# A state-space layer whose convolution becomes three shifted projections, with the row scaling moved to ScalarE

## The reference, cut to what matters

```python
xz = x @ W_in.T
u, z = jnp.split(xz, 2, axis=-1)
uc = conv(u over time, conv_w, 3 taps, padding 1, each of 256 channels by itself)
uc = silu(uc + conv_b)
...                                # delta, B and C from uc, a scan over time for 16 states
y = y * silu(z)
return y @ W_out.T

h = gelu(x_flat @ W1[e] + b1[e])   # for each of 8 experts e and the shared one
out = sum_e combine[e] * (h @ W2[e] + b2[e])
```

## Time and profile before

| what | value |
|---|---|
| runs | 2823.01, 2826.26, 2810.18 us, median 2823.01 |
| profiled execution | 2826.37 us, span 2824.6 us |
| granted TensorE clock over the span | 0.876 of full speed |
| start to the first step of loop 0 | 71 us |
| loops 0 to 3 | 71 to 937 us |
| rest of the mixture of batch 3 | 937 to 1097 us |
| attention | to about 2170 us |
| last layer | to the end |

### The profile page before, as it was taken

The page is one execution under the profiler, slowest core; times in us unless marked ns, Lnnn a source line. Parts: engine busy times, 40 slices in busy tenths (PEclk is TensorE's granted clock), DMA queues, the critical chain, the costliest instruction groups (busy, mean ns, idle before and its releaser), DMA issues.

```text
span 2824.6 us, 42372 instructions
## 1 busy us (share of the span) xinstructions
PE 2196.3 (78%) x15570; PEld 1492.3 (53%) x15570; DVE 2127.1 (75%) x3677; ACT 1699.0 (60%) x2627; POOL 1528.9 (54%) x1343
## 2 busy tenths in 40 slices
PE   2433788588589697989889888989896799739877
PEld 1101456255356475656556566656664568536665
DVE  4999978978978514999999999999998431572344
ACT  5353666477457344989888888888894134212422
POOL 0435323523433202878987887788788524553146
PEclk7555889698689898999999999999997899869988
DMA  3000000000000000110000000011010000000000
GB/s 108 0 0 0 1 0 1 1 1 1 19 1 1 18 6 12 34 25 23 24 24 24 24 24 23 24 30 28 24 35 23 1 1 1 1 15 1 1 1 16
DMA packets 32032, 42.06 MB, mean 15 GB/s; under 512 B 8897, under 2 KB 18130, under 8 KB 31442
## 3 DMA queue, kind: packets, MB, share of 16 engines
q1 hardware_dynamic: 31826, 39.34, 5.2%
HBM read 12.05 MB, written 2.10 MB: 5 GB/s over the span
## 4 chain that ended last, share of the span: by engine, by line
PE 37%; DVE 35%; ACT 12%; issue 8%; POOL 7%; SPq 0%; DMA 0%; POOLq 0%; ACTq 0%; DVEq 0%
DVE MA L1300 11%; PE ps L862 7%; DVE WB L1309 5%; PE ps L791 3%; ACT HR L763 3%; PE ps L793 2%; PE ps L792 2%; PE ps L1161 2%; PE ps L1132 2%; PE ps L1985 2%; DVE lnb L317 2%; DVE BIG L336 2%; ACT BIG L448 2%; DVE BIG L342 2%; PE ps L1144 2%
## 5 line engine op out<-in xcount | busy, mean ns | idle before, releaser
L1300 DVE TENSOR_REDUCE MA<-ps 128x1 f32<-128x1024 f32 x512 | 606.3, 1215 | 42.6 <-PE ps L1132 38.5
L420 POOL TENSOR_TENSOR MA<-MA,BIG 128x1024 f32<-128x1024 f32 x128 | 299.0, 2357 | 544.1 <-DVE BIG L342 544.1
L1228 ACT ACTIVATE WB<-ps,MA 128x1024 f32<-128x1024 f32 x461 | 513.4, 1117 | 114.9 <-DVE MA L1300 102.6
L1132 PE MATMUL ps<-BIG 96*128 96x512 f16 x1024 | 316.1, 391 | 95.3 <-ACT WB L1228 84.3
L1380 POOL TENSOR_SCALAR WB<-WB,MA 128x384 f32<-128x384 f32 x256 | 371.1, 1450 | 8.5
L862 PEld LDWEIGHTS ps<-WB,HR 128*128 128x128 f32 x2304 | 291.6, 202 | 33.8 <-issue 16.7
L862 PE MATMUL ps<-WB,HR 128*128 128x128 f32 x2304 | 300.4, 288 | 8.7 <-DVE acc L707 8.5
L763 ACT ACTIVATE HR<-ps,b 128x512 f32<-128x512 f32 x288 | 190.2, 686 | 148.9 <-PE ps L793 148.0
L1732 POOL TENSOR_TENSOR BIG<-MA,BIG 128x512 f32<-128x512 f32 x128 | 132.9, 1048 | 229.6 <-PE ps L1971 76.1
L1144 PE MATMUL ps<-ident,WB 128*128 128x128 f32 x1640 | 226.2, 282 | 9.8 <-DVE WB L1309 5.7
L1383 POOL TENSOR_TENSOR WB<-WB 128x384 f32<-128x384 f32 x205 | 209.3, 1021 | 17.1
(11 more groups left out here) (294 smaller groups left out, 4962.3 us busy)
## 6 DMA issues: line engine op xcount, KB each, us to landing
BIG<-BIG SPq DMA_DIRECT2D x192, 64.0 KB, 2.0
BIG<-MA SPq DMA_DIRECT2D x192, 64.0 KB, 2.0
WB<-w_dram SPq DMA_DIRECT2D x1, 2304.0 KB, 14.9
X<-x_dram SPq DMA_DIRECT2D x4, 512.0 KB, 12.6
HR<-w_dram SPq DMA_DIRECT2D x1, 2048.0 KB, 9.5
out_dram<-X SPq DMA_DIRECT2D x4, 512.0 KB, 3.2
BIG<-wqkv_dram SPq DMA_DIRECT2D x1, 1536.0 KB, 6.2
WB<-w_dram SPq DMA_DIRECT2D x2, 512.0 KB, 5.1
```

Of the source, the lines that this page charges most:

```text
L420: e.tensor_tensor(yy[:, c, :], yy[:, c, :], db[n % 2][c], ALU.add).then_inc(*p_my.up(b, n, c))
L1132: x = e.matmul(ps[s][:, 512 * h:512 * h + 512], stack[q % 2][0:96, 0, 2 * pp + s, 128 * i:128 * i + 128], stack[q % 2][0:96, 1, 2 * pp + s ...
L1228: e.activation(P_of(n, s), ps[s][:, :], ACT.Exp, bias=L[:, 2 * s + pp:2 * s + pp + 1], scale=1.0, accum_out=L[:, 4 + 2 * s + pp:5 + 2 * s ...
L1300: e.tensor_reduce(L_of(n)[:, c:c + 1], ps[s][:, :], AX, ALU.max, negate=True).then_inc(*v_amx.up(n, s))
```

## The change

**The convolution.** A new input `cwr` holds the taps as three rows, each broadcast to all partitions by a DMA of its own. At the start POOL multiplies the projection's weights with them into three sets of weights, `taps`. Each of the four tiles of u is then three matmuls that accumulate in PSUM, two of them on x shifted by one column; ACT copies the result with the bias straight into `cv`, and silu reads that. The padded buffers, the first tap on ACT and the two taps on DVE are gone. All four tiles of u now wait for both transposed halves.

**The row scaling.** In both layers `norms` on DVE becomes `normalized` on ACT (eight Identity activations with a scale and a bias per row), and POOL makes the bias: after the power, `scale_shift` adds a negation and a product. Four scalings per batch are moved, 16 in all. In the queues, new waits keep the statistics' buffer alive.

**The order.** All five tables of due times have new numbers.

```diff
+        taps = [x.rearrange("p a c -> p (a c)") for x in (lnp[:, 0:2, :], lnp[:, 2:4, :])]
+        taps.insert(1, winT[:, 0:256])
...
+        consts += [(BIG[:, 256 * k:256 * k + 256], d["cwr"][k:k + 1, :].partition_broadcast(128)) for k in range(3)]
...
         def const_pool(e):
...
+            e.wait_ge(s_c, S_C)
+            for k in (0, 2):
+                e.tensor_tensor(taps[k], winT[:, 0:256], BIG[:, 256 * k:256 * k + 256], ALU.mult).then_inc(*pool_own.up())
+            e.wait_ge(*pool_own.now())
+            e.tensor_tensor(taps[1], taps[1], BIG[:, 256:512], ALU.mult).then_inc(*p_const.up("taps"))
...
+        def scale_shift(e, s):
+
+            rstd(e, s).then_inc(*pool_own.up())
+            e.tensor_scalar(s[:, :, 7:8], s[:, :, 6:7], -1.0, None, ALU.mult).then_inc(*pool_own.up())
+            e.wait_ge(*pool_own.now())
+            return e.tensor_tensor(s[:, :, 8:9], s[:, :, 7:8], s[:, :, 9:10], ALU.mult)
+
+        def normalized(e, s, src, dst):
+            for j in range(8):
+                i = e.activation(dst[:, j, :], src[j], ACT.Identity, bias=s[:, j, 8:9], scale=s[:, j, 9:10])
             return i
...
         def front_dve(e, b):
...
-            yield in_at(b, "norm")
-            e.wait_ge(*p_mrs.at(b, "in"))
-            if b >= 2:
-                e.wait_ge(*p_mx.at(b - 2))
-            norms(e, st["m"], [tile_of(b, j) for j in range(8)], lnb[0]).then_inc(*v_mln.up(b, "in"))
-            for c in range(2):
-                yield in_at(b, f"conv{c}")
...
         def front_act(e, b):
+            yield in_at(b, "norm")
+            e.wait_ge(*p_mrs.at(b, "in"))
+            if b >= 2:
+                e.wait_ge(*p_mx.at(b - 2))
+            normalized(e, st["m"], [tile_of(b, j) for j in range(8)], lnb[0]).then_inc(*a_mln.up(b, "in"))
...
+                    e.activation(cv[c][:, 512 * h:512 * h + 512], path["u", b, c, h][0], ACT.Identity,
+                                 bias=small["convb"][:, c:c + 1], scale=1.0).then_inc(*a_m.up("u", b, c, h))
             yield in_at(b, "silu")
...
-                    e.wait_ge(*a_m.at("tr", b, h))
-                    e.matmul(bk, winT[:, 128 * c:128 * c + 128], xT[0][:, 512 * h:512 * h + 512], start=True,
-                             stop=True).then_inc(*t_m.up("u", b, c, h))
+                    if c == h == 0:
+                        for k in range(2):
+                            e.wait_ge(*a_m.at("tr", b, k))
...
+                    e.matmul(bk, taps[1][:, w], xT[0][:, 512 * h:512 * h + 512], start=True, stop=False)
+                    if h == 0:
+                        e.matmul(bk[:, 1:512], taps[0][:, w], xT[0][:, 0:511], start=False, stop=False)
+                        i = e.matmul(bk, taps[2][:, w], xT[0][:, 1:513], start=False, stop=True)
...
-LOOP_AT = {"tb": -3.75, "scan1": 2.72, "scan0": 4.94, "th": 7.2, "add": 9.43, "da": 0.34, "rows0": 4.86,
+LOOP_AT = {"tb": 0.1, "scan1": 2.12, "scan0": 3.92, "th": 7.37, "add": 10.11, "da": 0.14, "rows0": 5.09,
```

More of the change, by code:

```diff
@@ L212, in program @@
         v_const = Tick(sem("v_const"), keys(("aneg", "sel2"), ) + keys(("w1",), 9) + [("gw",), ("ones",)])
-        p_const = tick("p_const", ("half", "pad"))
+        p_const = tick("p_const", ("half", "taps"))
         def pieces():
@@ L424, in front_pool @@
             e.wait_ge(*v_mst.at(b, "in"))
-            rstd(e, st["m"]).then_inc(*p_mrs.up(b, "in"))
+            last = m_order.index((b, "in")) - 1
+            if last >= 0:
+                e.wait_ge(*a_mln.at(*m_order[last]))
+            scale_shift(e, st["m"]).then_inc(*p_mrs.up(b, "in"))
         def back_pool(e, b):
@@ L429, in back_pool @@
             e.wait_ge(*v_mst.at(b, "out"))
-            rstd(e, st["m"]).then_inc(*p_mrs.up(b, "out"))
+            last = m_order.index((b, "out")) - 1
+            if last >= 0:
+                e.wait_ge(*a_mln.at(*m_order[last]))
+            scale_shift(e, st["m"]).then_inc(*p_mrs.up(b, "out"))
             yield out_at(b, "x")
-            e.wait_ge(*v_mln.at(b, "out"))
+            e.wait_ge(*a_mln.at(b, "out"))
             xb = X[:, 8 * b:8 * b + 8, :]
@@ L524, in back_act @@
                              scale=1.0).then_inc(*a_m.up("out", b, h))
+            yield out_at(b, "norm")
+            e.wait_ge(*p_mrs.at(b, "out"))
+            normalized(e, st["m"], [lnb[0][:, j, :] for j in range(8)], lnb[0]).then_inc(*a_mln.up(b, "out"))
         def to(e, *p):
@@ L720, in moe_pool @@
             e.wait_ge(*v_fst.at(b, "in"))
-            rstd(e, st["f"]).then_inc(*p_frs.up(b, "in"))
+            if b:
+                e.wait_ge(*a_fln.at(b - 1, "out"))
+            scale_shift(e, st["f"]).then_inc(*p_frs.up(b, "in"))
             for k in routed if b in WEIGHTED else []:
@@ L731, in moe_pool @@
             e.wait_ge(*v_fst.at(b, "out"))
-            rstd(e, st["f"]).then_inc(*p_frs.up(b, "out"))
+            e.wait_ge(*a_fln.at(b, "in"))
+            scale_shift(e, st["f"]).then_inc(*p_frs.up(b, "out"))
             yield f_at(b, "x")
-            e.wait_ge(*v_fln.at(b, "out"))
+            e.wait_ge(*a_fln.at(b, "out"))
             xb = X[:, 8 * b:8 * b + 8, :]
@@ L738, in moe_act @@
         def moe_act(e, b):
+            yield f_at(b, "norm")
+            e.wait_ge(*p_frs.at(b, "in"))
+            if b:
+                e.wait_ge(*p_fx.at(b - 1))
+            normalized(e, st["f"], [tile_of(b, j) for j in range(8)], lnb[1]).then_inc(*a_fln.up(b, "in"))
             yield f_at(b, "tr", 1.2)
@@ L742, in moe_act @@
                 e.activation(xf[:, 0, 512 * h:512 * h + 512], bank[4 + h], ACT.Copy, scale=XS).then_inc(*a_fhi.up(b, h))
+            yield f_at(b, "rnorm")
+            e.wait_ge(*p_frs.at(b, "out"))
+            normalized(e, st["f"], [acc[:, j, :] for j in range(8)], lnb[1]).then_inc(*a_fln.up(b, "out"))
         def gate_act(e, b):
```

138 lines of the change are left out of this document (63 added, 75 removed).

## The result

| | before | changed |
|---|---|---|
| median of 14 runs each | 2819.0 us (2808.3 to 2827.4) | 2830.3 us (2826.0 to 2841.3) |
| profiled execution, its span | 2826.4, 2824.6 us | 2826.0, 2823.9 us |
| granted clock over the span | 0.876 | 0.893 |

The ratio is 1.0044 (95% interval 1.0029 to 1.0059): the change makes the kernel about 11 us slower. The forecast was 2823 us and no change. The time lies inside the stated range, but the interval of the ratio is clear of 1, so the forecast of "nothing" was wrong.

The account below looks back on a forecast made before the run. No engine bounds the whole: DVE bounds loop 0 and the loops' starts, a PE, ACT, DVE ping-pong the mixture stretches. Terms 4.5 - 3 + 9.6 - 17.6 + 5 + 1.8 = +0.3 gave 2823 us, range 2794 to 2848.

Parts of the forecast that it names:

- Term 1: Ahead of loop 0: longer chain through DMA issues, POOL, ACT's scaling and u's passes, +4.5 us, bounds +1 and +7.
- Term 2: Loop 0: DVE loses 7.8 us of work, 5 us open up from u; -3 us, bounds -8 and +5.
- Term 3: Starts of loops 1 to 3, to the split: chain +6.4, less DVE's savings; +3.8, +2.9, +2.9, together +9.6 us.
- Term 4: Mixture stretches of loops 1 to 3: shorter waits outweigh extra passes and scaling; -17.6 us, bounds -35 and 0.
- +4.1: Mixture stretch of loop 1: two further passes of a tile of u (2.04) ahead of down at two sums.
- Term 5: Behind the last loop: three scalings lie on the chain for which PE waits; +5 us, bounds +3 and +7.
- term 6: Start of the attention: first exponential later through ACT's scaling and the last power; +1.8 us, bounds 0 and 2.5.
- The step from trace to median: Whole kernel: sum added to the profiled 2826.4 us gives 2826.7; the median of the runs lies 3.4 lower, 2823.0.
- Rival A: All loops: DVE's work sets them, so its savings count in full; -29 us, 2794 us, chance 0.33.
- Rival B: Mixture stretches: tripled projection lies open, term 4 is 0; 2841 us, 2857 with u open in loops 1 and 2; chance 0.24.

Follow-up runs that it names:

- second trace: The changed kernel run once more with nothing altered: 2830.5 us, ratio 1.0049 to the kernel before.
- filler: Changed kernel plus four matmuls on constants, never read, ahead of the first down product of loops 1 and 2: 2813.0 us, 0.9971 to before.
- later scaling: Changed kernel with one number moved (norm 68.7 to 70.5), the front's scaling behind the second copy and a gelu: 2813.4 and 2814.4 us, 0.9997 and 0.9981.
- one-pass run: Changed kernel with one matmul per tile of u instead of three, shifted taps left out: 2805.1 us, 0.9963 to the kernel before.
- fast one: The kernel before, unchanged, run again for a third trace: 2810.2 us.

## Why the prediction was wrong

- **Term 1, ahead of loop 0** (+4.5; measured +3.6, and +5.9 in the second trace): right in size, by entries that cancel in part. Statistics start 1.7 us later, not 0.9 (21.30 for 19.56). POOL's negation and product took 0.26 and 0.21 us and put the scaling 0.6 us later, not 1.0. A scaling took 3.18 us, 3.2 worked out. By the Trainium skill, ScalarE: Activation LUTs, section What ACT_TABLE_LOAD costs, it was an estimated 3.1 us; the trace agrees (3.18).
- **Term 2, loop 0** (-3; -3.6): right, mechanism included; the opened waits are there (DVE waits 1.77, 0.30 and 2.59 us between 143 and 163 us, ahead of products and of bc1), and without the extra passes the loop is 4.8 us shorter, where I had judged 5.
- **Term 3, starts of the loops** (+9.6; +13.0): the mechanism holds. In loop 2 DVE waits 4.22 us for the addition into X and 5.25 for the split, where it had been busy throughout. The size was off there, +6.8 for +2.9 and beyond the bound of +6.4: of DVE's saving nothing counted.
- **Term 4, the mixture stretches** (-17.6; -11.9), is the step that failed. What it said of single waits was right: the 10.44 us at the third sum of loop 1 is gone (2.23 left at 363.37), and loop 3 gave 10.2 where 5.9 were forecast, since tb's wait fell from 10.33 to 1.80. Two entries were too small. The first is "the scaling stands between ACT's copies of the transposed weights, 3.2 and half a microsecond of waiting, +3.7". I priced that wait by its length and kept every duration behind it at the granted clock of the trace of before. The change took 11.6 us for down where before took 6.3, once in each of loops 1 and 2, 10.6 us together; the length itself was a fair bound (2.5 to the start of down, 2.4 behind it). The filler and the later scaling show it: they take 16 to 17 us off the median (13 to 22 by the ratios). That is more than the 10.6, because what follows at the next steps also falls on a better clock; how it divides I did not separate. The second entry is "+4.1" for the extra passes of u; the one-pass run gave 5.8 and 9.9 us back in these stretches of loops 1 and 2. The gains of the two runs overlap and can't be added, and no run has both edits.
- **Term 5, behind the last loop** (+5; +3.4), and **term 6** (+1.8; +1.9): right. What I missed between them is the attention's own table, worth 8 us to the change against the old one.
- **The step from trace to median** failed too. I set the sum against 2826.4 us and took 3.4 off, by three runs. Fourteen put the median 7.4 below that execution, which was of the slowest group. What a stage gains or loses depends on which execution of before it is read against: term 4 comes out at -11.9 against the slow one and at +5.7 against the fast one. The change had no executions below 2826 us. That it lost them by the low clock at the first down products is likely, since both edits that lift that clock bring times below 2810 back, but no trace follows it execution by execution.

Rival A (DVE sets the loops) is refuted: 47.6 us of DVE's work went for no gain. Rival B named the right sign, and its mechanism has a share: without the extra passes the kernel is 25 us faster. But it isn't the whole, for with all three passes in place the filled kernel is faster than before.

## What to carry to other kernels

A wait on TensorE's path can have two prices: its length, and the matmuls behind it at half the clock. When an edit puts new work of another engine (here 3.18 us) ahead of TensorE's next input, work the sum out with the following products at 1.2 GHz as well, since the rows don't tell beforehand whether the clock will fall. Look first whether the new instruction can stand one place later in its queue: here one number was worth 16 us. Before a difference of half a per cent is worked out against a trace, find out in which of the kernel's groups of times that trace lies.

## What the runs showed of the hardware

- Two executions of one program can repeat every start to 0.3 us through 1100 us (the repeats of before and of the moved scaling), or part by 15 us where the granted clock changes at another moment.
- The half clock at the first down product came behind waits of 3.86 and 4.55 us (change), 2.52 (before, loop 3) and 2.49 (one pass). It also came in the kernel before with the new tables, where the last long wait, of 2.94 us, had ended 3.5 us earlier. It did not come behind 3.42 us (change, at 310.72).
- POOL's instructions can take far longer beside DVE's scans. L321, 0.26 us alone, took 2.21 beside a scan that ran from 495.83 to 498.10. The pair L420 took 6.63 instead of 4.65 us while DVE's scan of 2.27 took 4.13.

```profile
495.93 2.21 POOL L321 TENSOR_SCALAR st_f<-st_f 128x8 f32<-128x8 f32 x1
506.26 0.26 POOL L321 TENSOR_SCALAR st_m<-st_m 128x8 f32<-128x8 f32 x1
506.77 6.63 POOL L420 TENSOR_TENSOR MA<-MA,BIG 128x1024 f32<-128x1024 f32 x2
507.13 4.13 DVE L351 TENSOR_TENSOR_SCAN BIG<-BIG 128x1024 f32<-128x1024 f32 x1
```

The Trainium skill, SBUF — State Buffer, section SBUF: two separate sides, says that VectorE and GpSimd share a port pair, which one of them holds for a whole instruction when the VectorE instruction reads two inputs from SBUF and the GpSimd one reads SBUF too. These rows agree (L321 ends at 498.14, just behind the scan; in the second case both end late, at 511.3 and 513.4), but no run here tried it alone.
